# One attention and mixture layer on one core: constants loaded in three pieces, idle products on a cleared tile, and a few small operations in another order in the first two steps

## The chip, the cores and the metric

The kernel runs on one core of a Trainium2 chip. The metric is the device time of one execution in microseconds; several unprofiled executions are timed and their median is given. One more execution is recorded by the hardware profiler. Five engines work side by side: TensorE (PE, matrix products; PEld is its weight load), VectorE (DVE), ScalarE (ACT), GpSimd (POOL) and SyncE (SP, which here only issues transfers). Each works through its own instruction list in order and waits on semaphores for the others.

## The reference

For 8 batches b of x (128 tokens, 512 columns), first attention with a paged cache (32 query heads, 8 key heads, width 128, 512 cached keys and 128 new ones), then a base layer with a mixture of low-rank experts:

```
q = rope(rmsnorm(x @ Wq.T) * q_norm_w, pos)      # pos = cache_seqlens + token
k = rope(rmsnorm(x @ Wk.T) * k_norm_w, pos);  v = x @ Wv.T
k_all = concat(k_cache[block_table], k);  v_all = concat(v_cache[block_table], v)
scores = q @ k_all.T * SCALE, cached keys at or past cache_seqlens set to -1e30
x = x + (softmax(scores) @ v_all) @ Wo.T
logits = x @ Wr.T + 5.0 * one_hot(language)       # top 2 of 8 experts, softmaxed
x = x + x @ W.T + 2.0 * sum_e gate_e * (x @ A_e.T) @ B_e.T
```

## The kernel before

Work is cut into 64 groups, g = head * 8 + batch; step s does the scores, softmax and transposes of group s, the product with the values and with Wo of group s - 1, and the projections and rotations that group s + 1 and s + 2 need. Every engine's order is written out by hand in functions of the same names on each engine. To keep float32 precision every operand of a product is split into a high part (ACT, a copy that rounds) and a low part (DVE, a subtraction, the helper `low` at L840), and `three_passes` (L314) issues high by high, low by high and high by low. The products have a 256 or a 512 column operand.

The places that matter here:

- Constants. `cst` holds, in this order, 64 inverse frequencies, the 128x128 identity matrix (`ident`, the second operand of every transpose), 8 expert numbers, the row number and the slot number. ACT issues its load (L773) right behind the load of the integers `cin` (L772).
- Start of PE. PE waits for the constants, issues 20 transposes of the identity into an unused bank (L1470, `WARM`), then the key and value projection of group 0 (it waits for `first_kv_low(0)` ahead of its first 6 products and for `first_kv_low(1)` ahead of the other 6), the query projection of group 0 (each quarter waits for `first_w_low(k)`), both for group 1, and the transposes of group 0.
- Start of DVE. With the constants it works out gather rows, positions, the angles `ang` (all are pieces of the tile `ps`), and their reduction by whole turns (`whole`, `turns`, `less_turns` twice), mixed with the low parts. The wrapper `tab` makes the next instruction wait until its own has ended. `split_x(c)` is the low part of x of batch c; the ACT function of this name is the high part. Then group 0 is scaled, squared, summed, and rotated: `times_sine` (tile `m2`, shown as m) and a product with the cosine.
- POOL does for each group the inverse norm (`meansq`, a power), `wr` = norm weights by inverse norm (L509), `rot` = u by cosine (L497), and two additions of `m` into `rot` (L515); DVE supplies `u` (L962) from `wr` and `m` (L916) from `u`. PE's `turn_queries` and `turn_new_keys` wait for the additions.
- Step 0 (`first_step`) on DVE: `sums_of_squares(1)`, `split_x(2)`, the mask of batch 0, then the row maxima (`rowmax`, L940), reciprocals of the row sums (`over_sum`, L947), `u` and `m` of group 1.
- Step 1. The first head's Wo is split in four: `first_wo_split(0..3)` on ACT (`wo_hi`) and DVE (`wo_lo`). The copy of the attention output o is `o_hi` on ACT and `o_lo` on DVE; PE's product with Wo waits for `o_lo`.

Of the kernel before, what the change touches and what calls it, by code (L numbers as in the profile page):

```python
# [16 lines left out]
P = 128  # L17
# [73 lines left out]
WARM = 20  # L91
# [6 lines left out]
def attention_lora(nc, xT, x, wqkv, wo, kv, normw, kpos, consts, ints, w1, wB, out):  # L98
    with ExitStack() as ctx:
# [101 lines left out]
        s_ints, s_cst, s_nw, s_kpos = sem("ints_landed"), sem("consts_landed"), sem("norms_landed"), sem("key_numbers_landed")  # L201
# [340 lines left out]
        def _(act):  # L542
# [170 lines left out]
            def step(s):  # L713
# [15 lines left out]
                if s == 1:  # L729
                    first_wo_split(3)  # L730
# [4 lines left out]
                if has(s):  # L735
                    if HB <= s + 3 < B:
                        split_x(s + 3)
                    exps(s, 2)
                    norm(s, 2)
                if has(s - 1):  # L740
                    wait(act, pe_o, s - 1)
                    wait(act, pe_y, s - 2)
                    nc.scalar.activation(o_hi[:], bank("O"), ACT.Copy).then_inc(a_o, 1)
                if has(s):

                    values(s)
                    probs(s, 0)
                    probs(s, 1)
                    probs(s, 2)
                    if s in W_MID:  # L750
                        w_split(W_MID[s])
                    if s in WO_MID:
                        wo_split(WO_MID[s])
                    exps(s, 3)
                    norm(s, 3)
                for n in W_AT.get(s, ()):
                    w_split(n)
                if has(g1):
                    turned_queries(g1)
                    cached_keys(g1)  # L760
                    new_keys(g1)
                for unit in ("QT", "KTC", "KTN"):
                    turn_x(s, unit)
# [9 lines left out]
            act.dma_start(cst[:], consts[:, :]).then_inc(s_cst, 16)  # L773
# [18 lines left out]
            queries(0)  # L792
            squares(0)
            sines()
# [43 lines left out]
        def _(dve):  # L838
# [126 lines left out]
            def first_step():  # L965
# [3 lines left out]
                over_sum(0, 0)  # L969
                rowmax(0, 2)  # L970
# [18 lines left out]
            def step(s):  # L989
# [32 lines left out]
                if s == 1:  # L1022
                    first_wo_split(3)
# [4 lines left out]
                if has(s - 1):  # L1028
                    wait(dve, a_o, s - 1)
                    low(o_lo[:], bank("O"), o_hi[:]).then_inc(d_olo, 1)  # L1030
                if s == G:
                    biased(3)
                    add_base(3)
                    dve.wait_ge(p_init, 2)
                    for b in range(HB):
                        largest(b)
                    gates(0)
                    final_turn(B - 2)
                    biased(4)
                    add_base(4)  # L1040
                    largest(4)
# [103 lines left out]
            def less_turns(part):  # L1145
# [7 lines left out]
            dve.wait_ge(s_cst, 16)  # L1153
# [4 lines left out]
                                        pos[:].unsqueeze(2).to_broadcast([P, B, HALF]), ALU.mult))  # L1158
            split_x(0)
            tab(nc.vector.tensor_scalar(whole, ang, float(1.0 / TWO_PI), None, ALU.mult))  # L1160
            first_kv_low(0)
            tab(nc.vector.tensor_copy(turns, whole))
            first_kv_low(1)
            first_w_low(0)
            first_w_low(1)
            less_turns(TWO_PI_A)
            first_w_low(2)
            first_w_low(3)
            split_x(1)
            less_turns(TWO_PI_B)  # L1170
# [27 lines left out]
            sums_of_squares(1)  # L1198
            split_x(2)
            dve.wait_ge(s_kpos, 16)  # L1200
            masks(0, 1)
            first_step()
# [30 lines left out]
        def _(pe):  # L1233
# [90 lines left out]
            def project_keys_values(g):  # L1324
                if g == 2:
                    wait(pe, a_kv, 1)
# [141 lines left out]
            pe.wait_ge(s_cst, 16)  # L1468
            for _ in range(WARM):
                nc.tensor.transpose(ps_s[:, 0, 0, 0:P], ident, ident)  # L1470
# [4 lines left out]
            project_keys_values(1)  # L1475
            turn_cached_keys(0)
# [93 lines left out]
```

## Time and profile before

| | |
|---|---|
| median of 3 unprofiled executions | 1165.25 us (1164.45 to 1165.65) |
| profiled execution | 1155.1 us |
| its span, first to last instruction | 1153.3 us |
| PE busy | 1139.4 us, 99% |
| DVE busy | 907.5 us, 79% |
| ACT busy | 925.4 us, 80% |
| POOL busy | 767.1 us, 67% |
| chain of work that ended last: share of PE | 95% |

The profiled execution is 10.15 us shorter than the median of the unprofiled ones, so a difference is what can be carried from one to the other, not a time. "Busy" of PE counts a matrix product until its modelled end, so that one which follows closely overlaps the one before it. In rows of the timeline the first number is the start, the second the duration, and what stands in brackets is the idle time of the engine ahead of the row and what ended it.

### The profile page before, as it was taken

The page shows a single profiled execution, that of the slowest core. Times are in us where ns is not written, and L with a number is a line of the kernel's source. Part 1 is how long each engine was busy: PE and PEld are TensorE (multiplying, and loading weights), DVE is VectorE, ACT ScalarE, POOL GpSimd, SP SyncE. Part 2 cuts the span into 40 slices and gives each one's busy share as a digit, 9 for nine tenths or more (in the row PEclk, how much of TensorE's full clock was granted, in tenths as well). Part 3 has the DMA queues.
Part 4 walks back from the last instruction along what each step waited for, and adds up shares of the span by engine and source line. Part 5 has one row for each costly group of instructions (what it writes and reads, how often), then busy time and mean ns, then how long its engine had stood idle before and what let it go on. Part 6 is the DMA issues. An engine that isn't in the chain of part 4 may idle for free.

```text
span 1153.3 us, 20952 instructions
## 1 busy us (share of the span) xinstructions
PE 1139.4 (99%) x6932; PEld 1027.3 (89%) x6932; DVE 907.5 (79%) x1883; ACT 925.4 (80%) x1833; POOL 767.1 (67%) x833
## 2 busy tenths in 40 slices
PE   7999999999999999999999999999999999999998
PEld 6788998998998998998999999899899899999997
DVE  7988888778778777777877877877777787777756
ACT  6888888888888888888888888888888888887751
POOL 5776776776676677667677677767766767767600
PEclk9999999999999999999999999999999999999999
DMA  7515322222222222322222222222222222221001
GB/s 244 164 62 156 105 73 88 90 67 87 89 78 79 92 79 72 93 87 63 92 91 64 87 90 76 81 92 76 74 92 82 67 90 88 63 80 56 19 1 74
DMA packets 56763, 98.12 MB, mean 85 GB/s; under 512 B 8784, under 2 KB 29136, under 8 KB 56528
## 3 DMA queue, kind: packets, MB, share of 16 engines
q1 hardware_dynamic: 44080, 63.08, 17.2%
q0 software_dynamic: 12288, 33.57, 10.0%
q8 instruction: 57, 0.93, 0.3%
q14 instruction: 50, 0.41, 0.1%
q10 hardware_dynamic: 288, 0.13, 0.1%
HBM read 90.45 MB, written 6.29 MB: 84 GB/s over the span
## 4 chain that ended last, share of the span: by engine, by line
PE 95%; DVE 2%; ACT 2%; issue 0%; DMA 0%; POOL 0%; ACTq 0%; DVEq 0%; POOLq 0%
PE ps_w L321 19%; PE ps_w L322 19%; PE ps_w L323 19%; PE ps_s L1368 19%; PE ps_w L1379 9%; PE ps_w L1347 2%; PE ps_w L1388 2%; PE ps_w L1354 2%; PE ps_s L1288 1%; PE ps_s L1322 1%; ACT ps L661 0%; PE ps_s L1470 0%; DVE m L916 0%; DVE y L1213 0%; DVE pt_lo L840 0%
## 5 line engine op out<-in xcount | busy, mean ns | idle before, releaser
L479 POOL DMA_INDIRECT kv_raw<-kv,rows x256 | 254.4, 994 | 93.3 <-issue 62.5
L667 ACT ACTIVATE ps<-ps,recip 128x640 f32<-128x640 f32 x256 | 212.9, 832 | 62.4 <-DVE recip L947 62.4
L840 DVE TENSOR_TENSOR pt_lo<-ps_w,pt_hi 128x512 fp32r<-128x512 f32 x322 | 204.3, 684 | 56.7 <-ACT pt_hi L672 54.5
L661 ACT ACTIVATE ps<-ps,negmax 128x640 f32<-128x640 f32 x256 | 212.7, 831 | 21.1 <-DVE negmax L940 20.9
L940 DVE CUSTOM_DVE_ANT_0 ps<-ps_s,mask 128x640 f32<-128x640 f32 x256 | 209.6, 819 | 4.1 <-PE ps_s L1368 0.3
L672 ACT ACTIVATE pt_hi<-ps_w 128x512 fp32r<-128x512 f32 x256 | 139.1, 598 | 74.0 <-PE ps_w L1379 74.0
L321 PE MATMUL ps_w<-w_hi,xt_hi 128*128 128x512 f32 (+1 forms) x496 | 172.6, 348 | 0.0
L322 PE MATMUL ps_w<-w_lo,xt_hi 128*128 128x512 f32 (+1 forms) x496 | 167.8, 338 | 0.0
L323 PE MATMUL ps_w<-w_hi,xt_lo 128*128 128x512 f32 (+1 forms) x496 | 167.7, 338 | 0.0
L497 POOL TENSOR_TENSOR rot<-u,cos 128x640 f32<-128x640 f32 x63 | 100.5, 1595 | 65.5 <-DVE u L962 65.5
L515 POOL TENSOR_TENSOR rot<-rot,m 128x320 f32<-128x320 f32 x126 | 107.8, 878 | 50.8 <-DVE m L916 50.7
L1379 PE MATMUL ps_w<-cst,ps 128*128 128x128 f32 x1024 | 133.2, 273 | 0.4 <-DVE qt_lo L840 0.3
L321 PE MATMUL ps_w<-pt_hi,v_hi 128*128 128x512 f32 x320 | 125.5, 392 | 0.0
L322 PE MATMUL ps_w<-pt_lo,v_hi 128*128 128x512 f32 x320 | 125.4, 392 | 0.0
L323 PE MATMUL ps_w<-pt_hi,v_lo 128*128 128x512 f32 x320 | 124.7, 390 | 0.0
L1368 PE MATMUL ps_s<-kt_hi,qt_hi 128*128 128x320 f32 x512 | 121.7, 319 | 2.2 <-DVE kt_lo L840 1.6
L1379 PEld LDWEIGHTS ps_w<-cst,ps 128*128 128x128 f32 x1024 | 117.2, 141 | 1.5 <-ACT ps L667 1.0
L1368 PE MATMUL ps_s<-kt_hi,qt_lo 128*128 128x320 f32 x512 | 116.8, 310 | 0.0
L1368 PE MATMUL ps_s<-kt_lo,qt_hi 128*128 128x320 f32 x512 | 116.4, 308 | 0.0
L321 PE MATMUL ps_w<-wo_hi,o_hi 128*128 128x512 f32 x256 | 105.5, 412 | 1.0 <-DVE o_lo L840 0.9
L916 DVE TENSOR_TENSOR m<-u,sin 128x640 f32<-128x640 f32 x64 | 104.6, 1634 | 0.2 <-ACT sin L602 0.2
L323 PEld LDWEIGHTS ps_w<-w_hi,xt_lo 128*128 128x128 f32 x496 | 93.6, 189 | 10.0
(186 smaller groups left out, 2609.4 us busy)
## 6 DMA issues: line engine op xcount, KB each, us to landing
xt_hi<-xsplit SPq DMA_DIRECT2D x56, 256.0 KB, 2.8
xt_lo<-xsplit SPq DMA_DIRECT2D x56, 256.0 KB, 2.8
w_raw<-wqkv SPq DMA_DIRECT2D x56, 192.0 KB, 2.4
wo_raw<-wo SPq DMA_DIRECT2D x56, 128.0 KB, 2.2
kv_raw<-kv,rows POOLq DMA_INDIRECT x256
y<-xT SPq DMA_DIRECT2D x8, 256.0 KB, 3.4
y<-x SPq DMA_DIRECT2D x8, 256.0 KB, 4.9
out<-y SPq DMA_DIRECT2D x8, 256.0 KB, 2.2
```

The source lines that it names most:

```text
L321: nc.tensor.matmul(out_ap, a_hi, b_hi, start=start and k == 0, stop=False)
L322: nc.tensor.matmul(out_ap, a_hi, b_lo, start=False, stop=False)
L323: last = nc.tensor.matmul(out_ap, a_lo, b_hi, start=False, stop=stop and k == n - 1)
L479: pool.indirect_dma_start(kv_raw[:, g % 2, t, :], None, kv[:, :], bass.IndirectOffsetOnAxis(rows[:, g % B, t:t + 1], 0)).then_inc(s_kv[g % ...
L515: nc.gpsimd.tensor_tensor(rot[:, :, a:a + HALF], rot[:, :, a:a + HALF], m2[:, :, c:c + HALF], ALU.add).then_inc(p_rot, 1)
L661: nc.scalar.activation(ps[:, h, :], ps[:, h, :], ACT.Exp, bias=negmax[:, s % 2, h:h + 1], scale=-1.0, accum_out=rowsum[:, s % 2, h:h + 1]) ...
L667: nc.scalar.activation(ps[:, h, :], ps[:, h, :], ACT.Copy, scale=recip[:, s % 2, h:h + 1]).then_inc(a_norm, 1)
L672: nc.scalar.activation(pt_hi[:, 0:CT, h, :], probs_bank(s, h).rearrange("p (t q) -> p t q", t=CT), ACT.Copy).then_inc(a_pt, 1)
L840: return nc.vector.tensor_tensor(out_ap, full, hi.bitcast(F32), ALU.subtract)
L940: nc.vector.tensor_tensor_reduce(out=halves(ps[:, h, :]), in0=ps_s[:, h % 2, :, 0:KH], in1=halves(mask[:, s % B, :]), scale=-SCALE, scalar ...
L1368: last = nc.tensor.matmul(ps_s[:, h % 2, half, 0:KH], a, c[:, half * KH:(half + 1) * KH], start=n == 0, stop=n == 2)
L1379: last = nc.tensor.transpose(probs_bank(s, h)[:, t * S:(t + 1) * S], ps[:, h, t * P:(t + 1) * P], ident)
```

## The change

Constants come in three loads: the 10 small columns, the 64 inverse frequencies, then the identity; DVE waits for the first two alone, PE for the identity only ahead of its first real transposes. PE's idle work becomes 14 plain float32 products of the tile `top` with itself; `top` is cleared by POOL at the start. DVE reduces the angles (`whole`, `turns`, both `less_turns`) ahead of the low parts of x and of the first weights. ACT takes the sine of group 0's angles ahead of the squares. `split_x(2)` on DVE goes from ahead of the mask to behind the first reciprocal of step 0, `sums_of_squares(1)` behind the mask, and PE gets a wait for it ahead of the keys and values of group 2. In step 1 `first_wo_split(3)` goes behind the copy of o on both engines, and `split_x(s + 3)` of steps 1 to 4 goes on ACT behind the copy of the new keys.

```diff
-WARM = 20
+WARM = 14
@@ ACT, step(s)
-                if s == 1:
-                    first_wo_split(3)
                 if has(g2):
                     queries(g2)
...
                 if has(s):
-                    if HB <= s + 3 < B:
-                        split_x(s + 3)
                     exps(s, 2)
                     norm(s, 2)
                 if has(s - 1):
...
                     nc.scalar.activation(o_hi[:], bank("O"), ACT.Copy).then_inc(a_o, 1)
+                if s == 1:
+                    first_wo_split(3)
...
                     new_keys(g1)
+                if HB <= s + 3 < B:
+                    split_x(s + 3)
@@ ACT, start
-            act.dma_start(cst[:], consts[:, :]).then_inc(s_cst, 16)
+            act.dma_start(cst[:, C_EXPERT:C_END], consts[:, C_EXPERT:C_END]).then_inc(s_small, 16)
+            act.dma_start(cst[:, 0:C_IDENT], consts[:, 0:C_IDENT]).then_inc(s_small, 16)
+            act.dma_start(ident, consts[:, C_IDENT:C_EXPERT]).then_inc(s_ident, 16)
...
             queries(0)
+            sines()
             squares(0)
-            sines()
@@ DVE, first_step
                 over_sum(0, 0)
+                split_x(2)
                 rowmax(0, 2)
@@ DVE, step(s)
-                if s == 1:
-                    first_wo_split(3)
                 if has(s):
                     over_sum(s, 2)
...
                     low(o_lo[:], bank("O"), o_hi[:]).then_inc(d_olo, 1)
+                if s == 1:
+                    first_wo_split(3)
@@ DVE, start
-            dve.wait_ge(s_cst, 16)
+            dve.wait_ge(s_small, 32)
...
+            tab(nc.vector.tensor_scalar(whole, ang, float(1.0 / TWO_PI), None, ALU.mult))
+            tab(nc.vector.tensor_copy(turns, whole))
             split_x(0)
-            tab(nc.vector.tensor_scalar(whole, ang, float(1.0 / TWO_PI), None, ALU.mult))
+            less_turns(TWO_PI_A)
             first_kv_low(0)
-            tab(nc.vector.tensor_copy(turns, whole))
+            less_turns(TWO_PI_B)
             first_kv_low(1)
-            first_w_low(0)
-            first_w_low(1)
-            less_turns(TWO_PI_A)
-            first_w_low(2)
-            first_w_low(3)
+            for k in range(KC):
+                first_w_low(k)
             split_x(1)
-            less_turns(TWO_PI_B)
...
-            sums_of_squares(1)
-            split_x(2)
             dve.wait_ge(s_kpos, 16)
             masks(0, 1)
+            sums_of_squares(1)
@@ PE
                 if g == 2:
+                    pe.wait_ge(d_xlo, g + 1)
                     wait(pe, a_kv, 1)
...
-            pe.wait_ge(s_cst, 16)
+            pe.wait_ge(p_init, 2)
+            idle = top[:].rearrange("p b n -> p (b n)")
             for _ in range(WARM):
-                nc.tensor.transpose(ps_s[:, 0, 0, 0:P], ident, ident)
+                nc.tensor.matmul(ps_s[:, 0, 0, 0:P], idle, idle, start=True, stop=True)
...
             project_keys_values(1)
+            pe.wait_ge(s_ident, 16)
             turn_cached_keys(0)
```

DVE's list at the start, before: from the angles to the low part of x of batch 1 (xt_lo; w_lo from w_raw is the key and value part, from wr, u, rot and m the four query quarters; ps<-ps are the angle operations).

```order
L1157 TENSOR_TENSOR ps<-cst,pos 128x512
L840 TENSOR_TENSOR xt_lo<-y,xt_hi 128x512
L1160 TENSOR_SCALAR ps<-ps 128x512
L840 TENSOR_TENSOR w_lo<-w_raw,w_hi 128x2x256
L1162 CAST ps<-ps 128x512
L840 TENSOR_TENSOR w_lo<-w_raw,w_hi 128x2x256
L840 TENSOR_TENSOR w_lo<-wr,w_hi 128x512
L840 TENSOR_TENSOR w_lo<-u,w_hi 128x512
L1146 SCALAR_TENSOR_TENSOR ps<-ps 128x512
L840 TENSOR_TENSOR w_lo<-rot,w_hi 128x512
L840 TENSOR_TENSOR w_lo<-m,w_hi 128x512
L840 TENSOR_TENSOR xt_lo<-y,xt_hi 128x512
```

The same place with the change (its `low` is at L842, its angle operations at L1149 and L1160 to L1163).

```order
L1160 TENSOR_TENSOR ps<-cst,pos 128x512
L1162 TENSOR_SCALAR ps<-ps 128x512
L1163 CAST ps<-ps 128x512
L842 TENSOR_TENSOR xt_lo<-y,xt_hi 128x512
L1149 SCALAR_TENSOR_TENSOR ps<-ps 128x512
L842 TENSOR_TENSOR w_lo<-w_raw,w_hi 128x2x256
L1149 SCALAR_TENSOR_TENSOR ps<-ps 128x512
L842 TENSOR_TENSOR w_lo<-w_raw,w_hi 128x2x256
L842 TENSOR_TENSOR w_lo<-wr,w_hi 128x512
L842 TENSOR_TENSOR w_lo<-u,w_hi 128x512
L842 TENSOR_TENSOR w_lo<-rot,w_hi 128x512
L842 TENSOR_TENSOR w_lo<-m,w_hi 128x512
```

Two 128x512 operations (L1149) now stand ahead of the second key and value part, where before one stood ahead of the third query quarter and one behind the list shown.

DVE's list in step 0 with the change, from the sum of squares of group 1 to u of group 1; here w_lo<-y,w_hi is the low part of x of batch 2, which before stood two rows ahead of the first L940 row (the first row maximum), with the mask between them.

```order
L909 TENSOR_REDUCE sumsq<-u 128x5
L942 ISA ps,negmax<-ps_s,mask 128x640
L942 ISA negmax 128x1
L942 ISA ps,negmax<-ps_s,mask 128x640
L942 ISA negmax 128x1
L949 RECIPROCAL recip<-rowsum 128x1
L842 TENSOR_TENSOR w_lo<-y,w_hi 128x512
L942 ISA ps,negmax<-ps_s,mask 128x640
L942 ISA negmax 128x1
L949 RECIPROCAL recip<-rowsum 128x1
L964 TENSOR_TENSOR u<-raw,wr 128x640
```

The low part of x now stands between the first reciprocal and the third row maximum.

DVE's list in step 1 with the change, from u of group 2 to the low parts of the transposed probabilities; wo_lo<-y,wo_hi is `first_wo_split(3)`, which before stood between u and the reciprocal.

```order
L964 TENSOR_TENSOR u<-raw,wr 128x640
L949 RECIPROCAL recip<-rowsum 128x1
L918 TENSOR_TENSOR m<-u,sin 128x640
L842 TENSOR_TENSOR o_lo<-ps_w,o_hi 128x512
L842 TENSOR_TENSOR wo_lo<-y,wo_hi 128x512
L942 ISA ps,negmax<-ps_s,mask 128x640
L942 ISA negmax 128x1
L842 TENSOR_TENSOR pt_lo<-ps_w,pt_hi 128x4x128 x3
```

It now stands between o_lo and the last row maximum of the step.

## Rows read from the trace of the kernel before

**Rows 1.** Waits of PE from 48 us to the end: total us, times, longest

```profile
PE ps_w L321 <- DVE o_lo L840: 0.9, 1, 0.9
```

**Rows 2.** Timeline, the start: start, duration, engine, line, operation

```profile
1.14 0.45 ACTq L773 DMA_DIRECT2D cst<-consts  x1
...
2.58 0.18 DVE L1150 CAST blkf<-cin 128x32 f32<-128x32 int32 x1 [1.72 <-DMA cin<-ints]
...
4.50 4.53 PE L1470 MATMUL ps_s<-cst 128*128 128x128 f32 x20 [4.50 <-DMA cst<-consts]
4.55 0.24 DVE L1154 TENSOR_SCALAR blkf<-blkf,cst 128x32 f32<-128x32 f32 x1 [1.38 <-DMA cst<-consts]
```

**Rows 3.** Timeline, DVE: second key and value part, and one less_turns

```profile
8.03 0.69 DVE L840 TENSOR_TENSOR w_lo<-w_raw,w_hi 128x512 fp32r<-128x512 f32 x1
...
9.84 0.69 DVE L1146 SCALAR_TENSOR_TENSOR ps<-ps 128x512 f32<-128x512 f32 x1
```

**Rows 4.** Chain that ended last: start, us per product, around PE's change of pace

```profile
9.46 0.21 PE ps_w L323
...
10.67 0.12 PE ps_w L322
...
10.91 0.23 PE ps_w L321
```

**Rows 5.** Timeline, group 0: query copy, squares, minus sines, m, transposes

```profile
13.69 0.60 ACT L627 ACTIVATE raw<-ps_w 128x512 f32<-128x512 f32 x1 [2.36 <-PE ps_w L323]
...
14.38 0.74 ACT L643 ACTIVATE wr<-raw 128x640 f32<-128x640 f32 x1
...
15.67 0.63 ACT L602 ACTIVATE sin<-sin 128x512 f32<-128x512 f32 x1
...
16.41 0.82 DVE L916 TENSOR_TENSOR m<-u,sin 128x640 f32<-128x640 f32 x1 [0.23 <-ACT sin L602]
...
19.82 0.66 PE L1347 MATMUL ps_w<-cst,rot 128*128 128x128 f32 x4 [1.58 <-ACT rot L804]
```

**Rows 6.** Timeline, step 0: DVE and POOL around the split of x2

```profile
21.95 0.81 DVE L907 TENSOR_REDUCE sumsq<-u 128x5 f32<-128x640 f32 x1
...
24.96 1.26 POOL L509 TENSOR_TENSOR wr<-nw,rstd 128x640 f32<-128x640 f32 x1
...
25.68 0.17 DVE L947 RECIPROCAL recip<-rowsum 128x1 f32<-128x1 f32 x1 [0.25 <-ACT ps L661]
...
25.93 0.82 DVE L940 CUSTOM_DVE_ANT_0 ps<-ps_s,mask 128x640 f32<-128x640 f32 x1
...
26.75 0.81 DVE L962 TENSOR_TENSOR u<-raw,wr 128x640 f32<-128x640 f32 x1
```

**Rows 7.** Timeline, POOL in step 2: first and last operation up to wr

```profile
57.46 0.20 POOL L489 TENSOR_SCALAR meansq<-sumsq 128x5 f32<-128x5 f32 x1 [0.69 <-DVE sumsq L907]
...
59.03 1.26 POOL L509 TENSOR_TENSOR wr<-nw,rstd 128x640 f32<-128x640 f32 x1
```

**Rows 8.** The page's groups: all rotations by the cosine, mean ns of one

```profile
L497 POOL TENSOR_TENSOR rot<-u,cos 128x640 f32<-128x640 f32 x63 | 100.5, 1595 | 65.5 <-DVE u L962 65.5
```

**Rows 9.** Timeline, step 1: Wo quarter, rotation, additions, last row maximum

```profile
44.53 0.68 DVE L840 TENSOR_TENSOR wo_lo<-y,wo_hi 128x512 fp32r<-128x512 f32 x1
...
44.68 1.95 POOL L497 TENSOR_TENSOR rot<-u,cos 128x640 f32<-128x640 f32 x1 [2.10 <-DVE u L962]
...
45.32 1.98 DVE L916 TENSOR_TENSOR m<-u,sin 128x640 f32<-128x640 f32 x1
...
47.45 1.70 POOL L515 TENSOR_TENSOR rot<-rot,m 128x320 f32<-128x320 f32 x2 [0.82 <-DVE m L916]
...
47.83 0.81 DVE L940 CUSTOM_DVE_ANT_0 ps<-ps_s,mask 128x640 f32<-128x640 f32 x1
```

**Rows 10.** Timeline: last operand of step 2's scores, and the scores

```profile
53.35 0.28 DVE L840 TENSOR_TENSOR kt_lo<-ps_s,kt_hi 128x128 fp32r<-128x128 f32 x1
...
54.06 0.54 PE L1368 MATMUL ps_s<-kt_hi,qt_hi 128*128 128x320 f32 x2
```

More of the change, by code:

```diff
@@ L197, in attention_lora @@
         ps_w = ctx.enter_context(nc.psum_tensor("ps_w", [P, NBANK, 512], F32))
-        s_ints, s_cst, s_nw, s_kpos = sem("ints_landed"), sem("consts_landed"), sem("norms_landed"), sem("key_numbers_landed")
+        s_ints, s_small, s_ident, s_nw, s_kpos = sem("ints_landed"), sem("small_consts_landed"), sem("identity_landed"), sem("norms_landed"), sem("key_numbers_landed")
         s_xt = [sem(f"x_transposed{n}_of_a_half_landed") for n in range(HB)]
```

## The prediction

> **What bounds the kernel now.** I read the waits of PE first, from 48 us to the end of the span. Only two are listed there; the larger is the product with Wo of step 1, which waits 0.9 us for the low part of o [rows 1], and the other is in the last steps, which the change doesn't touch. So from 48 us on PE works without a gap and only its own products count. The change removes none of those. It can then move the end in one way: by moving the moment at which PE becomes saturated. What counts is how much earlier or later PE starts the scores of step 2, at 54.06 [rows 10].
>
> Ahead of that moment PE waits for others, so I read the timeline of the first 56 us for the chain of who is late. PE starts when the constants land, at 4.50, and DVE with them, at 4.55 [rows 2]. The first key product follows PE's 20 idle transposes. Then the query product of group 0 releases ACT at 13.69, DVE multiplies by the sine at 16.41, and PE gets its first transposes at 19.82 after 1.58 us idle [rows 5]. In step 0 the chain is row maxima, u, rotation on POOL; in step 1 it is DVE, which from 48 to about 56 us has no gap to speak of. The times below are times of this trace; a shift that I found earlier is added at the end.
>
> **The start.** The load of the constants, 101 KB, was issued at 1.14 and took until 4.50, and each issue occupies ACT's queue 0.45 us [rows 2]. The second small load is thus issued at about 1.6. A load of 24 KB issued at 0.73 was used at 2.58 [rows 2], so the small ones cannot be there much ahead of 3.4; nor do I expect them behind 4.5. Large loads of x and weights share the engines, so I take 3.8 and keep both ends. DVE gains 0.75 us there.
>
> It does not give all of it to PE. The second key and value part started at 8.03 [rows 3], 3.48 behind DVE's start. Now two operations of 0.69 stand ahead of it, some 0.72 each with the hand-over that `tab` forces [rows 3], so it starts at 3.8 + 3.48 + 1.44 = 8.7 and ends at 9.4, 0.7 later than before. The first part ends two operations sooner, about 8.05. PE's first six products start there and the other six at 9.4; at 0.12 each [rows 4] they end at 10.15. The four query quarters are ready 0.6 apart from 10.0 on, faster than PE takes them (3 products of 0.23 [rows 4], 0.69 a quarter). 10.15 + 12 x 0.23 = 12.9, and with the drain of the last ACT starts its copy at about 13.1 instead of 13.69: 0.6 earlier. With loads at 4.5 it would be 0.1 later than now, at 3.4 it would be 1.0 earlier.
>
> ACT's copy of 0.60 is now followed by the sine, 0.62, and only then the squares, on which DVE's sum waits. Squares start at 13.1 + 0.6 + 0.6 = 14.3 instead of 14.38. From squares to the product with the sine took 16.41 - 14.38 = 2.03, of which the last 0.23 was a wait for the minus sines [rows 5]. Those end at 14.3 + 0.6 + 0.63 = 15.5 and no longer hold anything. 14.3 + 1.80 = 16.1, so DVE, and PE's first transposes behind it, come 0.3 earlier. The sine ahead of the squares costs about as much as it saves. Term: **-0.3** (bounds -0.8 and +0.2). The angles being ready sooner is worth nothing more, as ACT reaches the sine only behind the query copy.
>
> The idle products lie where PE has nothing to do, if they keep the fast pace up to the projections. Before, PE began at 4.50 and its products went from steps of 0.21 to 0.12 between 9.46 and 10.67 [rows 4], i.e. from the 1.2 to the 2.4 GHz level after some 5.4 us of work; the granted clock column says 1.00 for all this, so the steps are what shows it. Now PE can begin at about 1.0, when `top` is cleared. The 20 transposes took 4.53 us or 0.21 each [rows 2]; no row has a plain float32 product. If one costs two times a transpose, 14 last about 6 us, until 7.0, and the level is up near 6.4. I take that: a gap of one microsecond is left to 8.05. The Trainium skill ("FP8 and Floating Point Precision", TensorE Precision Notes) says that true FP32 makes four passes through the array, which by its count would be 0.43 us each at the low level; no run here shows it yet.
>
> **Step 0, the split of x2.** Ahead of the first row maximum there is 0.6 less work. The maximum starts at 23.3 rather than 23.86, its exponential follows, and the reciprocal stands at 25.2 instead of 25.68 [rows 6]. Then comes the moved split, a DVE operation with two operands in SBUF. What stands beside it is POOL's `wr`: sums of squares end at 22.54 + 0.81 = 23.35, as they started at 21.95 and the mask's 0.59 is now ahead [rows 6], and from there to `wr` POOL needs 59.03 - 57.46 and a hand-over of 0.1, or 1.66 [rows 7]. So `wr` runs from 25.0 to 26.27.
>
> How do the two share? In step 1 POOL's rotation ran from 44.68 to 46.63 and DVE's product, issued at 45.32, ended at 47.30, 0.67 behind POOL; POOL's took 1.95 where the mean is 1.595, as the Wo quarter was at work until 45.21 when it came [rows 8, 9]. Neither slows the other in part: the second waits until the first has ended, then does its work. The Trainium skill ("SBUF — State Buffer", Who interferes with whom) states this as an exclusive lock on a shared port pair between GpSimd and a DVE instruction with two SBUF inputs, held for the whole instruction; the trace agrees. By sharing without a lock the moved split would cost DVE 0.6 there and this term would be about zero; with the lock it is as follows.
>
> The split, ready at 25.24, finds `wr` at work, and ends at 26.27 + 0.54 = 26.81 (0.67 scaled from 640 to 512 columns). The third row maximum then starts at 26.77 instead of 25.93: **+0.84**. u, the sine product, POOL's rotation and additions and PE's transposes of group 1 all follow behind it in one line, so all of it stays. Should the split come first by a hair, `wr` ends at 27.15, u starts at 27.2 instead of 26.75, and the term is +0.45. Without any interference it is 0.0. PE's new wait is for this split: PE comes to it at about 26.2 and loses 0.6, but its transposes of group 1 wait for POOL anyway. I take 0.84.
>
> **Step 1.** Without the Wo quarter at 44.53 POOL's rotation runs 44.68 to 46.27 by its mean [rows 8], the sine product ends 0.67 behind it at 46.94 and not 47.30, and o_lo comes 0.36 earlier [rows 9]. That shortens the 0.9 us wait [rows 1]. But the quarter is now behind o_lo, at 47.46, again with two SBUF operands, and POOL's additions start 0.15 behind the sine product, at 47.1, the first until 47.95 (0.85, half of 1.70 [rows 9]). The quarter ends at 48.5, and the last row maximum, at 47.83 before, starts at 48.4: 0.57 later. DVE has no gap from there to the last operand of the next scores, 53.35 to 53.63, which PE takes up with a slack of 0.28, from 53.63 + 0.15 to 54.06 [rows 10]. So 0.36 is gained at a place where PE would wait again six microseconds later, and 0.57 - 0.28 = **+0.29** is lost. Bounds: without interference the row maximum is 0.25 late and the term is 0.0; no waiting at all would leave -0.36. ACT loses two operations of 0.6 ahead of its third exponential, which has waited behind them, but the sine product is tied to POOL, as worked out. `split_x` of steps 1 to 4 falls on ACT where it has about 1.2 us idle ahead of the last copies of probabilities (step 1), or where steps of 17 us leave ACT 2.7 us idle. I cost it at nothing, and at 0.6 if that cover were gone. In SP's queue the load of x7 waits for the last Wo quarter, 3 us more, and the next entry waits until 54 us anyway.
>
> **Sum.** -0.3 + 0.84 + 0.29 = +0.8 us on 1155.1, the same on the median: 1165.25 + 0.8 = 1166.1. About 2.3 us (0.2%) is what a measurement of this kernel can tell from no change, so this counts as no change.
>
> **Rivals.**
> - The reorderings do what they look like: no interference in either place, small constants at 3.4. -0.8 + 0.0 - 0.36 = -1.2 us: 1164.1. For it speaks that DVE does shed work ahead of two waits; against it that POOL's operations stand just where both splits go, as the pair of step 1 showed. Chance 0.22, within the same 0.2%.
> - The clock. If a product on the cleared tile costs 0.21 like a transpose, PE is done at 3.9 and idle for over 4 us; or cleared operands don't bring the level up. Then the projections start at 8.05 at the low level and need 5.4 us to leave it. Key part to 9.4 + 6 x 0.21 = 10.7; queries in steps of 0.43 until 13.5 (6.5 products), the other 5.5 at 0.23 to 14.75, 1.85 later than 12.9. Sum +0.8 + 1.85 = +2.65: 1167.9, slower. It decides once the low level lasts from 8.05 for about 5 us or more. Chance 0.07.
> - A large gain: PE is idle for only some 5 us between 4.5 and 48, and over 2.3 us of these would have to go. Nothing in the change reaches the 1.6 us ahead of the first scores. Chance 0.03.
> - Nothing moves: small loads land with the rest, splits fall beside POOL's gaps: within 0.3 us of now. Chance 0.18.
> - My forecast, +0.3 to +1.4: 0.50.
>
> **Numbers.** The range from 1164.0 to 1167.3 takes in both signs: the gain of 1.2 at one end, and at the other +0.2 + 0.84 + 0.29 + 0.6 = +1.9 with a little scatter, and leaves most of the clock case out. The forecast's own range is 1165.5 to 1166.7. Faster 0.03, same 0.89, slower 0.08 (the clock case and a crumb).
>
> **What would show it.** Small constants: DVE's second start near 3.8. Start: ACT's copy near 13.1, m near 16.1. Pace: 0.12 at the first key products. Step 0: w_lo from y of over 1 us beside POOL's `wr`. Step 1: w_o low of about 1 us beside POOL's additions, PE's wait for o_lo shorter, a new wait of 0.2 to 0.5 for the transposes or scores of step 2. I am wrong if PE idles for long at any other place behind 54 us, or if those two splits take 0.69.

## The result and the profile after

The changed kernel takes 1167.22 us, median of 17 executions (1165.21 to 1168.90); the kernel before took 1164.56 (1163.48 to 1165.65) beside it. The ratio is 1.0023, 95% interval 1.0016 to 1.0030: 2.7 us slower, where 0.8 was forecast. The time lies inside the predicted range, 0.1 us below its upper end, and outside the forecast's own, 1165.5 to 1166.7. The profiled execution took 1168.9 us.

The page after: span and instructions, busy times, granted clock in 40 slices, and the shares of the chain that ended last.

```profile
span 1167.1 us, 20971 instructions
...
PE 1150.7 (99%) x6940; PEld 1032.1 (88%) x6940; DVE 909.9 (78%) x1883; ACT 920.4 (79%) x1833; POOL 768.9 (66%) x833
...
PEclk8999999999999999999999999999999999999999
...
PE 91%; DVE 4%; ACT 2%; issue 2%; DMA 0%; POOL 0%; ACTq 0%; DVEq 0%; POOLq 0%
```

This span is 13.8 us above that of before. Most of that is not the change. One and the same kernel takes 1155 us on one chip and 1164.6 to 1165.2 on others (first experiment); the profile of before, at 1155.1, agrees with the first and its timed executions with the others, so I take them to come from different chips. So spans are compared below only between chips of one speed. Starts within the first 45 us can be compared across them: u of group 2 is at 43.8 and 43.9 in two traces of before on the fast side and at 44.2 with only the idle products changed on the slow side. What is new is the first digit of the clock row, 8, in the 29 us in which everything starts.

Timeline after, the start; it answers to [rows 2, 5].

```profile
1.02 5.69 PE L1472 MATMUL ps_s<-top 128*128 128x128 f32 x28 [1.02 <-POOL top L466]
1.14 0.45 ACTq L773 DMA_DIRECT2D cst<-consts  x1
...
1.61 0.51 ACTq L774 DMA_DIRECT2D cst<-consts  x1
...
5.85 0.24 DVE L1157 TENSOR_SCALAR blkf<-blkf,cst 128x32 f32<-128x32 f32 x1 [2.49 <-DMA cst<-consts]
...
9.45 0.69 DVE L842 TENSOR_TENSOR w_lo<-w_raw,w_hi 128x512 fp32r<-128x512 f32 x1
...
10.29 0.55 PE L321 MATMUL ps_w<-w_hi,xt_hi 128*128 128x256 f32 x1 [3.58 <-DVE w_lo L842]
...
17.40 0.60 ACT L627 ACTIVATE raw<-ps_w 128x512 f32<-128x512 f32 x1 [3.79 <-PE ps_w L323]
...
20.11 0.82 DVE L918 TENSOR_TENSOR m<-u,sin 128x640 f32<-128x640 f32 x1
...
23.61 0.63 PE L1348 MATMUL ps_w<-cst,rot 128*128 128x128 f32 x4 [1.63 <-ACT rot L806]
```

Read it downwards against [rows 2, 5]. DVE's second start is 1.3 us later than before although it needs less data; PE's idle products end at 6.71 and PE waits 3.58 us for the first low part of the weights; the copy of the queries of group 0 starts 3.7 us later, m 3.7, PE's first transposes 3.8. Up to the transposes the delay is the one at the copy. It is made of two parts: the first key product starts 1.6 us later (10.29 for 8.68), and from there to the copy PE takes 7.1 us in place of 5.0. Step 0 adds another 0.8: u of group 1 starts at 31.39, where [rows 6] have 26.75.

The windows of after and of before, in this order: stretch, its length, busy time of PE, PEld, DVE, ACT and POOL with instruction counts, granted clock, DMA share and GB/s.

```profile
9.00:12.40 3.40, 2.11 (x10) 2.14 (x11) 3.33 (x6) 1.52 (x3) 2.79 (x3) 0.54 0.47 156
12.40:20.00 7.60, 7.60 (x29) 6.21 (x29) 4.80 (x8) 2.98 (x6) 1.44 (x2) 0.76 0.52 155
20.00:32.00 12.00, 8.78 (x54) 8.36 (x53) 9.78 (x23) 9.73 (x21) 8.26 (x8) 0.86 0.72 237
```

```profile
9.00:12.40 3.40, 3.40 (x21) 3.10 (x20) 3.37 (x7) 2.08 (x4) 2.74 (x3) 1.00 0.57 188
12.40:20.00 7.60, 6.02 (x36) 5.13 (x35) 6.68 (x14) 6.16 (x12) 3.45 (x4) 1.00 0.60 171
```

Before, the granted clock reads 1.00 throughout. This column misses the low level from which PE starts: four of before's key products, from 9.04 to 9.9, also came in steps of 0.21 to 0.22, with 1.00 in the column. After, it is at the 1.2 GHz level for most of 9 to 16 us, right when PE has the projections to do: all its key products come in steps of 0.21 us, and the query products until 16.0 in steps of 0.43, in place of 0.12 and 0.23 [rows 4]. From 12.4 to 20 PE is busy all of the time with 29 instructions; before it did 36 in 6.02.

### The profile page after: what moved, and what is told of

Same layout as the page of the kernel before. It is cut to its first block, busy times and chain, and to the rows that moved or that the text cites. A ratio compares the mean times of both kernels' runs of the same rounds, so it can differ in the third digit from the quotient of the medians.

```text
span 1167.1 us, 20971 instructions
## 1 busy us (share of the span) xinstructions
PE 1150.7 (99%) x6940; PEld 1032.1 (88%) x6940; DVE 909.9 (78%) x1883; ACT 920.4 (79%) x1833; POOL 768.9 (66%) x833
## 3 DMA queue, kind: packets, MB, share of 16 engines
q1 hardware_dynamic: 44080, 63.08, 17.2%
## 4 chain that ended last, share of the span: by engine, by line
PE 91%; DVE 4%; ACT 2%; issue 2%; DMA 0%; POOL 0%; ACTq 0%; DVEq 0%; POOLq 0%
PE ps_w L321 18%; PE ps_s L1369 18%; PE ps_w L322 18%; PE ps_w L323 18%; PE ps_w L1380 9%; PE ps_w L1348 2%; PE ps_w L1389 2%; PE ps_w L1355 2%; ACT ps L661 1%; PE ps_s L1288 1%; DVE m L918 1%; PE ps_s L1322 1%; DVE pt_lo L842 0%; DVE ps L942 0%; ACT ps L667 0%
## 5 line engine op out<-in xcount | busy, mean ns | idle before, releaser
L842 DVE TENSOR_TENSOR pt_lo<-ps_w,pt_hi 128x512 fp32r<-128x512 f32 x322 | 204.7, 683 | 53.5 <-ACT pt_hi L672 36.7
L321 PEld LDWEIGHTS ps_w<-w_hi,xt_hi 128*128 128x128 f32 x496 | 94.4, 190 | 11.7 <-issue 3.7
```

The source lines that it names most:

```text
L321: nc.tensor.matmul(out_ap, a_hi, b_hi, start=start and k == 0, stop=False)
L842: return nc.vector.tensor_tensor(out_ap, full, hi.bitcast(F32), ALU.subtract)
```

## The experiments

**The kernel before, once more; the start alone; the steps alone; 32 idle products.** These four ran on one chip. First the edits of the two halves, shortened: the start alone has the three loads, the idle products, DVE's new order and the sines ahead of the squares; the steps alone have the moved splits and the mask:

```diff
 # start only
+            act.dma_start(cst[:, C_EXPERT:C_END], ...); act.dma_start(cst[:, 0:C_IDENT], ...); act.dma_start(ident, ...)
 # steps only
+                split_x(2)              # between over_sum(0, 0) and rowmax(0, 2)
+                if s == 1:
+                    first_wo_split(3)   # behind o_lo
 # after, with
-WARM = 14
+WARM = 32
```

> The kernel before, once more, for its profile. In the trace of the changed kernel PE's period of 17.05 us is 17.32 in about every second step (the product with Wo waits for o_lo), 8.8 us in all, and in the first trace of the kernel before it never is. Theory slips-are-common: the median of before (1164.56) is 9.5 us over its profiled execution because an ordinary execution of it has the same slips; then this profile is near 1164 and has some 25 to 35 steps of over 17.2 us. Rival, slips-from-the-change: the change brings them; then this trace has none, and its span is near 1153.

Measured 1154.92 us, against 1155.05 for before on this chip (ratio 0.9999, 0.9990 to 1.0008). It agrees with the first profile, 1155.1, and not with the 1164.56 of the result. Neither of the two readings that I had set against each other holds as it stood: the longer steps are no part of an ordinary execution on this chip, and the kernels below that lack the change show them on the other chips. So chips differ, by 9.5 us for the very same program. "Faster chip" below is this one; "slower" are the one of the next experiment and the one of the last.

> Only the start of the change: three loads, 14 products on the cleared tile, angles first, sines ahead of squares; steps 0 and 1 as before. Theory start: the small loads land at about 5.8, PE idles over 3 us and works at the low clock level until about 16, so the transposes of group 0 start near 23.6 and the time is 2 to 4.5 us over before. Rival, port (the loss is the moved splits of steps 0 and 1 that wait for POOL): -0.5 to +0.5 us against before.

Measured 1158.76 against 1155.05, ratio 1.0033 (1.0020 to 1.0045). The start alone costs 3.7 us, more than the whole change on the slower chips.

> Only the moves of steps 0 to 4; the start as before. Theory start: within 1 us of before on either side. Rival, port: +1.1 us (0.84 for the split of x2 behind POOL's wr, 0.29 for the Wo quarter behind POOL's first addition), with the two splits taking over 1 us in the trace. If the moves save what they seem to save: -0.5 to -1.2 us.

Measured 1155.41 against 1155.05, ratio 1.0002 (0.9993 to 1.0011): +0.4 us, which the interval doesn't tell from nothing; the trace is read below.

> The changed kernel with 32 idle products and not 14, which bridge PE's gap from 6.7 to 10.3 us. Theory clock: the first key products run in steps of 0.12, ACT's copy of the queries of group 0 starts near 14.5 and not 17.4, the low level at 26 to 30 us may go too; 2.5 to 3.5 us less than the changed kernel, i.e. near before. Rival, DVE: the late constants alone hold the start (the weights' low parts are ready only from 12.1 on), so at most 1 us is won.

Measured 1157.93 against 1155.05, ratio 1.0023 (1.0014 to 1.0032), 0.8 less than the start alone, though this kernel has the moves of steps 0 to 4 as well. The whole change with 14 idle products did not run on this chip. Windows of the start alone, then the last of them in before again, and the timeline of the kernel with 32 idle products:

```profile
9.00:12.40 3.40, 2.92 (x13) 2.96 (x14) 3.37 (x7) 1.65 (x3) 2.48 (x4) 0.50 0.48 152
12.40:20.00 7.60, 7.40 (x40) 6.20 (x39) 6.01 (x11) 5.11 (x9) 2.59 (x2) 1.00 0.54 163
20.00:32.00 12.00, 8.96 (x46) 8.78 (x47) 9.47 (x24) 8.15 (x19) 8.24 (x8) 0.72 0.72 254
```

```profile
20.00:32.00 12.00, 10.47 (x56) 9.28 (x56) 10.37 (x22) 9.48 (x20) 8.41 (x9) 0.86 0.68 241
```

```profile
1.02 10.26 PE L1472 MATMUL ps_s<-top 128*128 128x128 f32 x64 [1.02 <-POOL top L466]
...
5.30 0.24 DVE L1157 TENSOR_SCALAR blkf<-blkf,cst 128x32 f32<-128x32 f32 x1 [2.01 <-DMA cst<-consts]
...
11.04 0.36 PE L321 MATMUL ps_w<-w_hi,xt_hi 128*128 128x256 f32 x1
```

The low clock sits in the start, and comes twice. Against before again the start alone has DVE's second start 0.7 us later, the first key product 1.5 later (9.48 for 8.01), the copy 2.4 (15.24 for 12.84), and u of group 1 3.0 (29.78 for 26.80). The 0.9 between key product and copy goes with the low level until 12.4; the last 0.6 goes with the second one, which lasts from 22.7 to 29.5 where before again has it from 21.2 to 24.4. The second and third row maximum then wait 0.65 and 0.69 us for scores that come at the low pace.

With 32 products there is no idle time ahead of the projections, and the first of them come at full pace (0.28 for 256 columns instead of 0.41), but the idle work now lasts until 11.0 and itself holds the projections: the copy starts at 15.49, against 15.24 in the start alone. One loss was traded for another.

**The parts of the start.** Four kernels on a slower chip, before at 1164.74: the change again; the change with the ten small columns and the frequencies side by side, in one load of 74 columns; before with only the idle products on the cleared tile; that with the one small load.

```diff
 # one small load
-C_IDENT = C_INVF + HALF
-C_EXPERT = C_IDENT + P
+C_EXPERT = C_INVF + HALF
+C_IDENT = C_SLOT + 1
+            act.dma_start(cst[:, 0:C_IDENT], consts[:, 0:C_IDENT]).then_inc(s_small, 16)
+            act.dma_start(ident, consts[:, C_IDENT:C_END]).then_inc(s_ident, 16)
 # idle products only, in before
+            pe.wait_ge(p_init, 2)
+                nc.tensor.matmul(ps_s[:, 0, 0, 0:P], idle, idle, start=True, stop=True)   # x 14
```

> The changed kernel once more. If the chip is of the kind on which before takes 1155: theory start: the start-only kernel cost 3.7 us and the steps-only kernel 0.4, so about 3.0 to 4.1 us over before, with few steps of over 17.2 us. Rival, slips-from-the-change: over 9 us, as its first trace read against the first trace of before would have it.

Measured 1167.03, ratio 1.0020 (1.0011 to 1.0029): the result repeats. DVE's second start was at 4.92 in this trace, the first key product at 9.37, the copy at 15.24.

> The changed kernel, but the small constants lie side by side and come in one load of 74 columns, issued where the single load stood; the identity behind it. Theory two-loads (the second issue, 0.47 us later, puts the last small one behind the loads of x and weights): DVE starts at 3.4 to 4.0 instead of 5.0 to 5.9, PE's first key product comes 1.2 to 2 us earlier, and the time is 1.5 to 3 us below the changed kernel. Rival, queue (the engines are full whatever is asked first): DVE starts at 4.5 or later, under 1 us is won.

Measured 1165.55, ratio 1.0006 (0.9997 to 1.0015), 1.5 us less than the change with its two small loads. DVE starts at 4.11 and the first key product at 8.55, both 0.8 earlier, but in the two profiled executions the copy gains only 0.1 (15.11): with the one load the clock falls at 9.8, behind the sixth key product. So the traces do not show where the 1.5 of the medians lies.

> The kernel before, with only its 20 idle transposes replaced by the 14 products on the cleared tile and PE's wait for the constants put ahead of its first real transposes. Theory clock: PE's gap is now only from 6.7 to about 7.6, the level stays up, first key product near 7.6 in steps of 0.12; the query copy 0.5 to 1.0 us earlier, time 0 to -1.0 us against before. Rival: a dip to the low level after the gap, then +0.5 to +2.

Measured 1164.50, ratio 0.9997 (0.9988 to 1.0006). The idle products on the cleared tile neither win nor lose anything that this can tell.

> g3 and one load of the 74 small columns ahead of the identity; orders all as before. Theory two-loads: DVE starts at 3.4 to 4.0, first key product 6.8 to 7.2, time 0.8 to 1.8 us below before, and this is the best version. Rival, queue: as g3 within 0.3 us.

Measured 1164.24, ratio 0.9997 (0.9988 to 1.0006). One small load and DVE's old order: no loss. Its timeline:

```profile
1.02 5.05 PE L1472 MATMUL ps_s<-top 128*128 128x128 f32 x28 [1.02 <-POOL top L466]
...
4.06 0.24 DVE L1155 TENSOR_SCALAR blkf<-blkf,cst 128x32 f32<-128x32 f32 x1 [0.98 <-DMA cst<-consts]
...
7.31 0.35 PE L321 MATMUL ps_w<-w_hi,xt_hi 128*128 128x256 f32 x1 [1.24 <-DVE w_lo L841]
...
12.50 0.60 ACT L627 ACTIVATE raw<-ps_w 128x512 f32<-128x512 f32 x1 [1.76 <-issue]
```

The small constants are there at 4.06, PE waits 1.24 us, the key products run in steps of 0.12, and the copy starts at 12.50, 1.2 earlier than in [rows 5], though only 0.3 earlier than in before again. With two small loads DVE started at 5.85, 4.92, 5.04 and 5.30 in four traces, with one at 4.06 to 4.28 in six, with the single load of everything at 4.22 to 4.74 in four (before's 4.55 among them; mean 4.47). So DVE gets its constants some 0.3 us earlier if they are split off in one load, and 0.4 to 1.4 later if in two.

**DVE's order, and the clock filled up.** Four kernels on a third chip, again a slower one, before at 1165.17. All have one small load and the idle products. The first adds DVE's new order (angles ahead of the low parts), the second this with 22 idle products. The third has the old order and 7 and 6 more products on the cleared tile where PE waits, ahead of the first query transposes and of the first scores; the fourth is the third with the change's moves in steps 0 to 4.

```diff
 # fill, in the third and fourth
             turn_cached_keys(0)
+            for _ in range(7):
+                nc.tensor.matmul(ps_s[:, 0, 0, 0:P], idle, idle, start=True, stop=True)
             turn_queries(0)
             turn_new_keys(0)
+            for _ in range(6):
+                nc.tensor.matmul(ps_s[:, 0, 0, 0:P], idle, idle, start=True, stop=True)
```

> g4 (one small load, 14 idle products, orders as before) with DVE's angle operations ahead of the low parts, as in the change. Theory angles: the first key and value part is ready 1.2 us later, PE's gap grows to about 2.4 us, and a dip to the low level follows at 9 to 13 us: query copy 2 to 2.8 us later than in g4 (12.5), time 1.5 to 3 us over g4. Rival: the angle order alone is harmless (0.7 us on the second part), at most 0.8 us over g4.

Measured 1167.60, ratio 1.0021 (1.0013 to 1.0030): DVE's order alone costs 2.9 us, each kernel taken against its own before. The first key product comes at 8.66, not 7.31, the copy at 13.66, not 12.50. That is 1.2 us of the 2.9. The profiled execution, 1165.48, was the shortest of the eleven and shows no low clock at 9 to 16 us; the others were up to 2.9 us longer. Their granted clock over the whole execution is 0.995 to 0.997, and 0.999 in the profiled one, so the low level lasted longer in them; that it was in the projections is likely, and not shown.

> h1 with 22 idle products, which last until about 8.3, so that PE has no gap. Theory clock: no dip at 9 to 13 us, the query copy 1.5 to 2 us earlier than in h1, time 1 to 2 us below h1; what is left over g4 is the angle order itself, 0.4 to 1.0 us. Rival DVE: the copy comes as late as in h1.

Measured 1166.05, ratio 1.0009 (1.0000 to 1.0017), with the copy at 13.68. Eight more idle products, which leave less idle time ahead of the projections, take 1.6 us off the median and narrow the executions to 1165.1 to 1167.0. The granted clock of its executions is 0.997 to 0.999. This fits the reading above: about 1.6 of the loss is clock, and the rest, 1.3, the later low parts.

> g4 with 7 more products on the cleared tile ahead of the first query transposes and 6 ahead of the first scores, where PE waits 1.8 and 1.6 us. Theory clock: the dip at 21.6 to 25.0 us, which before has too, goes; from the first transposes to u of group 1 takes 6.9 us and not 7.6 us, time 0.5 to 1.0 us below g4. Rival: the dip stays or only moves, or the extra products delay the scores: -0.2 to +0.5.

Measured 1164.29, ratio 0.9992 (0.9983 to 1.0001). The fill keeps the clock up: the window from 20 to 32 us reads 1.00 where the same kernel without it reads 0.86. And it gains nothing that can be told: u of group 1 starts at 26.48 with it and at 26.43 without. That is not because the low clock was free there. From PE's first scores to u of group 1 it takes 4.6 us in the first trace of before, the one without the fall, and 5.3 in before again, with it, and 6.0 in the start alone, where the fall lasts longest. With the fill it takes 5.1: the first row maximum starts 2.2 us behind the first scores, against 1.7 in the first trace of before, and PE then waits 1.10 us for `negmax`. What holds that maximum is open; the view names PE's scores, but shows those of its own head ended 1.1 us before.

> h3 with the change's moves in steps 0 to 4. With full clock at the first scores the split of x2 should meet POOL's wr. Theory port, as predicted: the split takes over 1 us, u of group 1 comes 0.45 to 0.84 us later than in h3, scores of step 2 another 0.3 us later, time +0.7 to +1.1 over h3. Rival, slack: the split takes 0.67 as in f3 and the sum is +0.2 to +0.4.

Measured 1162.97, ratio 0.9980 (0.9971 to 0.9989): the one kernel that is faster than before beyond doubt, by 2.2 us, and some 4 us faster than the change was on the other slower chip. One of its twelve executions took 4882.87 us and is not in the ratio; no other kernel had one like it, and what it was stays open.

## Why it came out as it did

**The time fell inside the range by luck.** The difference of 2.7 us is that of the clock case, +2.65, which the range was meant to leave out for the most part. It is inside because before itself came out at 1164.56 and not at the 1165.25 on which the range was built. The working gave +0.8, and its mechanism of the start was wrong, as follows. The 2.3 us that I called no change was too wide as well: the intervals here reach about 1 us to either side with eleven executions or more, and 2.7 is a loss clear of noise.

**PE as the bound from 48 us on: held on the faster chip, with a limit on the slower ones.** The kernel with the fill and the moves shows two waits of PE from 44 to 57 us, of 0.5 and 0.3. What was lost was lost ahead of that: the start alone is 3.0 us behind before again at u of groups 1, 2 and 3 alike, and 3.3 at the end. On the slower chips PE does wait behind 57 us, 1.7 us for `o_lo` in the changed kernel, and that is where the moves of steps 1 to 4 count, below.

**"Small constants at 3.8, bounds 3.4 and 4.5": failed.** They were used at 4.92 to 5.85, outside the bounds. I had taken the price of a small load from its bytes and its place in the queue. ACT's queue has two issues for what DVE needs, at 1.14 and 1.61; the chain after gives 4.14 us from the second to its landing, where all 101 KB came in 3.36 before [rows 2]. What delays the second is not shown: no run separates its place in the queue from its shape. That two small loads are the loss, and not the splitting off, is shown by the change with the one load (DVE 0.8 earlier, -1.5 us).

**"First part ends two operations sooner, at 8.05": right in its working, wrong in what it was held against.** From DVE's second start to the first part, two operations ahead of the end of the second, I had 4.25; to the first key product it took 4.44 and 4.45 in the two traces of the change. Before it was 4.13, and 3.25 with the idle products and the old order: PE's transposes had hidden that the low part was ready earlier. The new order therefore costs 1.2 us against what was to be had. And the 8.68 from which I counted a gain of 0.6 was high: in before again the same transposes took 3.94 us and not 4.53, the key products ran at full pace, and the first one started at 8.01.

**"A gap of one microsecond": failed, and with the late start of DVE this is the step that made the size.** The idle products lasted about as predicted (6 us; 5.69), 0.41 us a product. The Trainium skill ("FP8 and Floating Point Precision", TensorE Precision Notes) has true FP32 in four passes; the trace agrees, with 28 matrix instructions for 14 products and about 0.4 us for each product, nearly all at the 1.2 GHz level. But the gap behind them was 3.6 us, not 1, and the clock, which had come up (the shortest of the 28 takes 275 ns, the median 421), was down again at the first projections. The clock rival (0.07) thus gave the outcome, though by another door: I had tied it to products that end too early or do not bring the clock up, and had not asked what it does when everything behind them is late. The 5.4 us that I gave the low level were those of one trace: here it held the projections from 10.3 to 16.0, in the start alone from 9.5 to 12.4. Its price, 1.85 us, was about right: from the first key product to the copy the change takes 2.1 us more than before, and 1.6 came off a median with 22 products in place of 14. In the start alone the first key product is 1.5 late and the two low stretches add 0.9 and 0.6; that is 3.0 of the 3.3 by which the profiled executions differ (3.7 in the medians), where my term was -0.3. That the clock case's sum, +2.65, met the 2.7 is in part chance: it has my +0.8 in it, two of whose three terms were wrong.

**The sine ahead of the squares: free.** From the copy to m is 2.71 us after, 2.72 before and 2.80 in before again; I had 3.0.

**Step 0, "+0.84": the collision failed, the split costs +0.42.** Timelines of the fill kernel without the moves and then with them (same start):

```profile
23.58 0.82 DVE L941 CUSTOM_DVE_ANT_0 ps<-ps_s,mask 128x640 f32<-128x640 f32 x1 [0.57 <-PE ps_s L1369]
...
26.48 0.81 DVE L963 TENSOR_TENSOR u<-raw,wr 128x640 f32<-128x640 f32 x1
```

```profile
23.59 0.82 DVE L941 CUSTOM_DVE_ANT_0 ps<-ps_s,mask 128x640 f32<-128x640 f32 x1 [1.17 <-PE ps_s L1370]
...
24.15 1.26 POOL L509 TENSOR_TENSOR wr<-nw,rstd 128x640 f32<-128x640 f32 x1
...
25.41 0.16 DVE L948 RECIPROCAL recip<-rowsum 128x1 f32<-128x1 f32 x1 [0.24 <-ACT ps L661]
25.49 0.67 DVE L841 TENSOR_TENSOR w_lo<-y,w_hi 128x512 fp32r<-128x512 f32 x1
...
26.90 0.81 DVE L963 TENSOR_TENSOR u<-raw,wr 128x640 f32<-128x640 f32 x1
```

The sentence "the maximum starts at 23.3 rather than 23.86" failed. DVE sheds 0.6 of work, and the maximum starts no earlier: it now waits 1.17 instead of 0.57 for PE's scores, which I had not looked at as the next in line. The reciprocal stays where it was, and `wr` is done at 25.41, 0.08 ahead of the split. So the split finds POOL's `wr` finished, takes its usual 0.67, which I had named as a sign of being wrong, and there is no collision. What is left is the split itself on the path, less the time that DVE had to spare. The pair without the fill, before again and the steps alone, shows the same: the wait of the first maximum grows from 0.45 to 1.03, the split takes 0.67, and u comes 0.47 later behind the copy.

**Step 1, "+0.29" from the lock: the mechanism held.** The same two kernels, without and with the moves:

```profile
44.42 1.95 POOL L497 TENSOR_TENSOR rot<-u,cos 128x640 f32<-128x640 f32 x1 [2.11 <-DVE u L963]
...
47.19 1.71 POOL L515 TENSOR_TENSOR rot<-rot,m 128x320 f32<-128x320 f32 x2 [0.83 <-DVE m L917]
47.57 0.81 DVE L941 CUSTOM_DVE_ANT_0 ps<-ps_s,mask 128x640 f32<-128x640 f32 x1
47.75 0.47 PE L321 MATMUL ps_w<-wo_hi,o_hi 128*128 128x512 f32 x1 [0.89 <-DVE o_lo L841]
```

```profile
44.84 1.57 POOL L497 TENSOR_TENSOR rot<-u,cos 128x640 f32<-128x640 f32 x1 [2.11 <-DVE u L963]
...
47.23 2.15 POOL L515 TENSOR_TENSOR rot<-rot,m 128x320 f32<-128x320 f32 x2 [0.82 <-DVE m L917]
47.61 1.03 DVE L841 TENSOR_TENSOR wo_lo<-y,wo_hi 128x512 fp32r<-128x512 f32 x1
47.79 0.47 PE L321 MATMUL ps_w<-wo_hi,o_hi 128*128 128x512 f32 x1 [0.51 <-DVE o_lo L841]
...
48.57 0.81 DVE L941 CUSTOM_DVE_ANT_0 ps<-ps_s,mask 128x640 f32<-128x640 f32 x1
...
53.52 0.63 PE L1381 MATMUL ps_w<-cst,ps 128*128 128x128 f32 x4 [0.32 <-DVE qt_lo L841]
```

The rotation starts 0.42 later (step 0's delay) but takes 1.57, not 1.95, so o_lo is 0.38 earlier in its frame and PE's wait falls from 0.89 to 0.51. Then the quarter starts at 47.61 and POOL's first addition, half of 1.71, ends at 48.08; the quarter ends at 48.64, 0.56 behind that. POOL's pair takes 0.44 longer. The last row maximum is 1.00 later, 0.42 of it inherited, 0.58 its own, against 0.57 forecast; and a new wait of 0.32 for the transposed queries appears, within the predicted 0.2 to 0.5. The Trainium skill ("SBUF — State Buffer", Who interferes with whom) calls it an exclusive lock on the port pair; the trace agrees, in both directions.

By the steps alone these moves cost 0.4 us together on the faster chip, where I had 1.13. Behind the copy u of group 1 is 0.5 later than in before again and u of group 3 0.8; by u of group 8 0.45 of that is back, which I had not foreseen.

**Steps 1 to 4, "costed at nothing": wrong, most of all on the chips of the result.** On the slower ones the moves give more time back than they cost. Windows from 58 to 142 us of the fill kernel without and with the moves, and the waits of PE in that stretch of the first:

```profile
58.00:142.00 84.00, 82.73 (x500) 73.63 (x499) 67.06 (x137) 69.62 (x140) 57.84 (x63) 1.00 0.31 98
```

```profile
58.00:142.00 84.00, 84.00 (x515) 75.75 (x514) 70.11 (x140) 71.79 (x146) 60.50 (x65) 1.00 0.33 104
```

```profile
PE ps_w L321 <- DVE o_lo L841: 1.1, 2, 0.6
```

Without the moves PE waits twice for o_lo in this stretch and does 15 instructions fewer; with them it doesn't wait at all. The first product with Wo of step 8 follows that of step 1 by 121.9 to 122.6 us in the five kernels without the moves on the slower chips and by 120.5 to 121.3 in the four with them; on the faster chip it is 119.6 to 119.7 without and 119.9 with them. The times are 1164.29 and 1162.97. Of these 1.3 us about 0.8 is there at step 8; where the rest comes from is open. ACT has `split_x` of steps 2 to 4 ahead of its exponentials in the old order, which fits; that it is these and not the quarter of step 1 is argued, as no run has one of the moves alone.

So an estimate for the chips of the result is +3.7 at the start, measured on the faster chip, and -1.3 for the moves, measured beside the fill: +2.4, against 2.3 to 2.7 for the whole change. Neither half was measured alone on a slower chip. My +0.8 was -0.3 and +1.13.

## What to carry to other kernels

When an operation is taken from ahead of a wait, ask first who releases the wait: DVE's 0.6 us in step 0 became 0.6 us of waiting. Don't price a small load by its bytes alone: one small load came 0.3 us earlier than the big one, two came 0.4 to 1.4 later. Warm-up work on PE is lost if what follows it comes late; work out first when the first real product can start, and let the warm-up end there. A baseline trace is one execution: the two of before differ by 0.7 us at the first key product and by nothing at u of group 1. And check a gain of this size on the chip that it will be timed on.

## What the runs showed of the hardware

Chips differ by 0.8% on one kernel: 1155.05 us on one chip, 1164.74 and 1165.17 on two others, with operations as long on both sides (the exponentials 0.83 us, the rotation by the cosine 1.60 and 1.61). Windows from 142 to 1100 us of the kernel before on the faster, and of the kernel with the idle products alone on a slower one; then DVE's waits for scores of the two from 200 to 900 us (total, times, longest):

```profile
142.00:1100.00 958.00, 957.90 (x5849) 864.85 (x5848) 758.12 (x1528) 792.89 (x1567) 668.62 (x723) 1.00 0.26 79
```

```profile
142.00:1100.00 958.00, 956.13 (x5800) 858.47 (x5799) 753.50 (x1515) 783.82 (x1560) 669.07 (x723) 1.00 0.26 79
```

```profile
DVE ps L940 <- PE ps_s L1368: 0.3, 1, 0.3
```

```profile
DVE ps L940 <- PE ps_s L1368: 17.1, 20, 0.9
```

On the slower chip PE does 49 instructions fewer in the same 958 us, at 0.164 us each 8.0 us. The loss comes in nearly every second step, 17.3 in place of 17.05 us: from step 9 to the end 21 to 23 steps of over 17.2 us in each trace on the slower chips, none or one on the faster, the last few steps left out. DVE then waits 0.9 us for scores in 20 steps of 41, which it does once, for 0.3, on the other chip. The granted clock is 1.00 on both. What makes the steps alternate is open, and so is whether it belongs to the chip or to something else that differed with it.

The granted clock falls behind short idle times, and not each time. In the start alone PE had waited 2.9 us and the clock was at the low level from 9 to 12.4; with one small load in the change 1.6 us of waiting was followed by it at 9.8, in the profile of DVE's order alone 2.6 us was not. And in all traces without the fill but the first profile of before it fell once more, behind the two waits ahead of the first scores, somewhere between 21 and 30 us (0.86 from 20 to 32, 0.72 in the start alone). That second fall is not free. Of before's executions on the two slower chips, the 26 whose granted clock is 1.000 took 1164.5 and 1164.8 us in the mean, the other 42 1165.0 and 1165.4.
